# Turning row maxima into shift rows: a transposing DMA in place of TensorE transposes and a VectorE copy

## What is computed

```python
qkv = (x @ Wqkv.T + bqkv).reshape(Bb, Ss, 3, H, HD).transpose(2, 0, 3, 1, 4)
q, k, v = (qkv[0], qkv[1], qkv[2])
attn = jax.nn.softmax(jnp.einsum('bhid,bhjd->bhij', q, k) / jnp.sqrt(jnp.float32(HD)), axis=-1)
...
out = jnp.einsum('bhij,bhjd->bhid', mod, v).transpose(0, 2, 1, 3).reshape(Bb, Ss, Ee)
return out @ Wout.T + bout
```

## Time and profile before

| | |
|---|---|
| median of 3 runs | 988.95 us |
| lowest and highest | 984.64 and 991.41 us |
| the profiled execution | 985.31 us, span 983.5 us |
| mean granted share of the TensorE clock | 0.974 |

### The profile page before, as it was taken

How to read it: one execution, slowest core, us unless ns; L and a number is a source line. 1 busy time by engine, 2 the same in 40 slices (tenths; PEclk the granted TensorE clock), 3 DMA queues, 4 the chain that set the end, 5 groups by cost and what they waited for, 6 DMA issues and landing times. The chain is left out here.

```text
span 983.5 us, 24019 instructions
## 1 busy us (share of the span) xinstructions
PE 910.8 (93%) x6978; PEld 548.8 (56%) x6979; DVE 743.0 (76%) x1546; ACT 536.0 (54%) x1104; POOL 622.0 (63%) x761
## 2 busy tenths in 40 slices
PE   6799999999999999998878998989999999999993
PEld 3233333333333343332314777878888888888882
DVE  7688889898998999899886886685655665655652
ACT  3167787788778777875677653223233233233230
POOL 4314345546556555532445699889988878788785
PEclk9799999999999999998989999999999999999997
DMA  6553171714518162450365896834334334333332
GB/s 214 103 87 77 35 117 56 133 53 89 131 35 163 55 102 64 79 98 13 120 184 161 258 254 180 184 56 73 63 57 55 44 55 55 44 56 54 44 57 30
DMA packets 106768, 93.10 MB, mean 95 GB/s; under 512 B 60025, under 2 KB 99321, under 8 KB 104385
## 3 DMA queue, kind: packets, MB, share of 16 engines
q1 hardware_dynamic: 92000, 71.98, 31.9%
q0 software_dynamic: 14304, 19.15, 12.3%
q10 hardware_dynamic: 384, 0.97, 0.3%
HBM read 49.46 MB, written 38.68 MB: 90 GB/s over the span
## 5 line engine op out<-in xcount | busy, mean ns | idle before, releaser
L1232 DVE TENSOR_REDUCE mx<-bank 128x1 f32<-128x512 f32 x512 | 327.4, 682 | 45.2 <-PE bank L802 40.3
L1122 ACT ACTIVATE arena<-bank 128x512 f32<-128x512 f32 x512 | 277.7, 596 | 70.7 <-PE bank L813 67.0
L1155 ACT ACTIVATE hf<-bank,small 128x256 f32<-128x256 f32 x316 | 133.6, 471 | 262.5 <-PE bank L987 216.5
L677 POOL TENSOR_TENSOR hl<-hf,hh 128x256 f16<-128x256 f32 x316 | 236.5, 1114 | 56.2 <-DVE y_dest L1471 40.8
L1454 DVE CAST hh<-hf 128x256 f16<-128x256 f32 x316 | 178.7, 597 | 114.1 <-ACT hf L1155 108.0
L987 PE MATMUL bank<-hh,arena 128*128 128x256 f16 x1248 | 210.8, 275 | 9.2 <-POOL hl L677 8.2
L802 PE MATMUL bank<-arena 48*128 48x512 f16 x512 | 167.0, 393 | 13.9 <-DVE mx L1232 10.7
L987 PE MATMUL bank<-hl,arena 128*128 128x256 f16 x624 | 171.7, 275 | 0.0
L813 PE MATMUL bank<-arena 49*128 49x512 f16 x512 | 163.2, 388 | 8.5 <-ACT arena L1122 5.8
L685 POOL DMA_INDIRECT out<-y,y_dest x78 | 128.5, 1648 | 20.7 <-issue 17.6
L987 PEld LDWEIGHTS bank<-hh,arena 128*128 x1248 | 122.6, 98 | 32.6 <-issue 14.6
(11 more groups left out here) (215 smaller groups left out, 982.0 us busy)
## 6 DMA issues: line engine op xcount, KB each, us to landing
raw<-in_we SPq DMA_DIRECT2D x16, 1024.0 KB
arena<-parts_dram SPq DMA_DIRECT2D x84, 128.0 KB
parts_dram<-arena SPq DMA_DIRECT2D x64, 128.0 KB, 3.7
xs<-in_pads SPq DMA_DIRECT2D x8, 816.0 KB
arena<-in_xT SPq DMA_DIRECT2D x8, 512.0 KB, 4.6
arena<-in_x SPq DMA_DIRECT2D x8, 512.0 KB, 5.9
out<-rows SPq DMA_DIRECT2D x8, 512.0 KB, 5.0
arena<-parts_dram SPq DMA_DIRECT2D x24, 64.0 KB, 3.0
```

The costliest lines, as they stand in the source:

```text
L677: nc.gpsimd.tensor_tensor(hl[which][:, par, m, :], hf[which][:, m, :], hh[which][:, par, m, :], ALU.subtract).then_inc(lo[which], 1)
L1122: nc.scalar.activation(pr[:, s % TT, n, :], b_bank[no % B_RING][:, :], ACT.Exp, scale=SCALE).then_inc(b_read, 1)
L1155: nc.scalar.activation(hf[which][:, m, :], layer[which][m // 2][:, m % 2 * TS:(m % 2 + 1) * TS], ACT.Relu, bias=bias[which][:, bass.ds(e, ...
L1232: V.tensor_reduce(mx[:, g % 2, s % TT, c:c + 1], a_bank[no % A_RING][:, :], X, ALU.max).then_inc(a_read, 1)
```

## The change

The maxima are laid out as 16 adjacent columns, head by head, in a tile padded with zeros to 128 columns. SP turns that 128 x 128 tile by one transposing DMA from SBUF to SBUF, so that column (head, block) becomes a partition of 128 values, waits for it, and stores eight such partitions to each half of the stack. The four transposes on PE, their use of a PSUM bank and the copy on DVE are gone, and `shift` is [128, 2, 128] in place of [4, 2, 512].

```diff
     i, ahead = SHIFTS_AT[s % SLOTS]
     b = s // SLOTS + ahead
-    return [("mt", i, b)] if 0 <= b < B else []
+    return [(i, b)] if 0 <= b < B else []
...
-    order = [t for s in range(FIRST, LAST) for t in shift_task(s) + tasks(s)]
+    order = [t for s in range(FIRST, LAST) for t in tasks(s)]
...
-    shift = carve(b3_words[:, S + E + VW:S + E + VW + S].bitcast(F16), 0, [G, 2, S])
+    shift = carve(b3_words[:, S + E + VW:S + E + VW + P].bitcast(F16), 0, [P, 2, P])
...
-    mx = sb("mx", [P, 2, TT, G])
-    mxp = sb("mxp", [P, 2, TT, G], F16)
+    mx = sb("mx", [P, 2, G, TT])
+    mxp = sb("mxp", [P, 2, P], F16)
...
         def store_shift(g, b):
-            evicted(sp, ("mt", g, b))
+            n = b * NG + g
+            sp.wait_ge(mx_split, n + 1)
+            sp.wait_ge(bank_cleared, 2)
+            if n >= 2:
+                sp.wait_ge(shift_in, 32 * (n - 1))
+            sp.dma_start(shift[:, g % 2, :], mxp[:, g % 2, :], transpose=True).then_inc(shift_turned, 16)
+            sp.wait_ge(shift_turned, 16 * (n + 1))
             for half in range(2):
                 r = half * ROW_HALF + STACK
-                sp.dma_start(q[r:r + 1, b % 2, 2 * g:2 * g + 2, :], shift[2 * half:2 * half + 2, g % 2, :])\
+                sp.dma_start(q[r:r + 1, b % 2, 2 * g:2 * g + 2, :], shift[half * 2 * TT:(half + 1) * 2 * TT, g % 2, :])\
                     .then_inc(shift_in, 16)
...
-            elif what == "mt":
-                turned_shift = m[0:G, 0:S // 2].bitcast(F16)
-                for t2 in range(TT):
-                    last = nc.tensor.transpose(turned_shift[:, t2 * P:(t2 + 1) * P], mxp[:, i % 2, t2, :], ident[:, :])
...
-            for t in shift_task(s):
-                product(t)
             scores(s, (2, 3))
...
         def split_maxima(g):
             dve.wait_ge(a_read, (g + 1) * TT * G)
-            V.tensor_scalar(mxp[:, g % 2, :, :], mx[:, g % 2, :, :], -1.0 / SHIFT_UNIT, None, ALU.mult).then_inc(mx_split, 1)
+            if g >= 2:
+                dve.wait_ge(shift_turned, 16 * (g - 1))
+            V.tensor_scalar(mxp[:, g % 2, 0:G * TT], mx[:, g % 2, :, :].rearrange("p h t -> p (h t)"), -1.0 / SHIFT_UNIT, None, ALU.mult)\
+                .then_inc(mx_split, 1)
...
-            elif what == "mt":
-                if b * NG + i >= 2:
-                    dve.wait_ge(shift_in, 32 * (b * NG + i - 1))
-                V.tensor_copy(shift[:, i % 2, :], m[0:G, 0:S // 2].bitcast(F16)).then_inc(done, 1)
...
         V.memset(pv_bank[:, :], 0.0).then_inc(bank_cleared, 1)
+        V.memset(mxp[:, :, G * TT:P], 0.0).then_inc(bank_cleared, 1)
```

More of the change, by code:

```diff
@@ L365, in model @@
     a_ready, a_read, b_ready, b_read = sem("a_ready"), sem("a_read"), sem("b_ready"), sem("b_read")
-    mx_split, shift_in = sem("mx_split"), sem("shift_in")
+    mx_split, shift_turned, shift_in = sem("mx_split"), sem("shift_turned"), sem("shift_in")
     slots_free, out_copied = sem("slots_free"), sem("out_copied")
@@ L499, in _ @@
             for t in shift_task(s):
-                store_shift(t[1], t[2])
+                store_shift(*t)
             if s == 1 - SLOTS:
@@ L861, in inputs_ready @@
                 pe.wait_ge(vpart_set, b + 1)
-            elif what == "mt":
-                pe.wait_ge(mx_split, b * NG + i + 1)
-                pe.wait_ge(cleared, 11)
             elif what == "ot":
@@ L1231, in reduce_head @@
             c = column(head_of(n, True))
-            V.tensor_reduce(mx[:, g % 2, s % TT, c:c + 1], a_bank[no % A_RING][:, :], X, ALU.max).then_inc(a_read, 1)
+            V.tensor_reduce(mx[:, g % 2, c, s % TT:s % TT + 1], a_bank[no % A_RING][:, :], X, ALU.max).then_inc(a_read, 1)
         def split_maxima(g):
             dve.wait_ge(a_read, (g + 1) * TT * G)
-            V.tensor_scalar(mxp[:, g % 2, :, :], mx[:, g % 2, :, :], -1.0 / SHIFT_UNIT, None, ALU.mult).then_inc(mx_split, 1)
+            if g >= 2:
+                dve.wait_ge(shift_turned, 16 * (g - 1))
+            V.tensor_scalar(mxp[:, g % 2, 0:G * TT], mx[:, g % 2, :, :].rearrange("p h t -> p (h t)"), -1.0 / SHIFT_UNIT, None, ALU.mult)\
+                .then_inc(mx_split, 1)
         def newton(r, t, m):
@@ L1520, in _ @@
             for t in shift_task(s):
-                split_maxima(t[2] * NG + t[1])
+                split_maxima(t[1] * NG + t[0])
             if scored(s + LEAD):
@@ L1524, in _ @@
                 reduce_head(s + LEAD, 1)
-            for t in shift_task(s):
-                take(t)
             if (at, 0) in ROUTE_AT and 0 <= b - 1 < B:
```

## The result

The changed kernel takes 1003.27 us in the median of four runs (997.98 to 1006.68); the kernel before, beside it on the same chip, 988.31 us (984.64 to 991.41). The ratio is 1.0161, with a 95% interval of 1.0124 to 1.0198: it is 1.6% slower. The profiled execution is the quickest of the four, 997.98 us, its span 996.1 against 983.5 us.

The account below looks back on a forecast made before the run. PE was taken to bound the middle of the attention, DVE close behind. Terms -6.4 - 1.9 - 2.0 + 5.4 - 1.8 = -6.7 us, from 988.9 to 982.2 us; range 974 to 996.

Parts of the forecast that it names:

- The place and the mechanism: Slot 6's transposing DMA queues behind the next batch's stack reads, so PE waits at slot 8, not at 0, 4, 12.
- Rival D: Every group: SBUF-to-SBUF transposing DMA has a longer fixed time; PE waits from 3.5 us on; about 1005 to 1032 us; chance 0.15.
- rival C: Slot 8: wait over 2 us as transposing DMA and stores each queue; six batches x 2.5 us; 994 us; chance 0.15.
- the size of the wait at slot 8: PE waits 1.1 us in batch 4, 0.9 us in the mean over six batches, 5.4 us in all.
- +5.4 -1.8: Slot 8 waits over six batches cost 5.4 us, of which a third, 1.8 us, is taken as given back.
- the 1.8 us given back: While PE stands at slot 8, DVE and ScalarE catch up, so the waits of slots 11 and 12 shrink.
- The fixed times: With free queues: transposing DMA 1.8 us (0.3 for the signal), stores 2.1, plus 0.1; chain 4.0 us from the maxima.
- 6.4 us: PE, slots 2, 6, 10, 14: removing the transposes saves 0.20 us in each of 32 groups.
- 2.0 for VectorE: Removing DVE's copy saves 0.33 us once in each of six middle batches, at slots 11 and 12; 2.0 us.
- The last line of the prediction: Sign of being wrong: a DVE that paces the attention would cut PE's 6.4 us saving and raise DVE's 2.0.
- The waits for the maxima ahead of the transposes: PE idled 2.9 us in two waits before L947; 1.0 us comes back as a wait, so 1.9 us saved.
- order in SyncE's queue: Slot 6: each engine takes one queue's descriptors in ring order, so the transposing DMA lands behind the reads, at 311.7 us.

## Why the prediction was wrong

The forecast was 982.2 us, with a range up to 996; the time is 1003.3. Point by point, by its own steps.

**The place and the mechanism: right.** Everything was to hang on slot 6's transposing DMA meeting the stack reads, with one PE wait at slot 8, and no wait at slots 0, 4 and 12. So it is. Rival D, a transposing DMA that is slow in every group, is out: 2.27 us with free engines, under the 3.5 from which it would decide. It is rival C, the wait at slot 8 over 2 us, that came, and harder than it was priced.

**The step that failed: the size of the wait at slot 8,** 0.9 us in the mean. The waits sum to 15.5 us in six batches, 2.6 in the mean, and slots 7 and 8 together lost 18.8 us, 3.1 a batch, where +5.4 -1.8 stood in the sum. Of the 1.8 us given back, 0.7 is seen: behind the three long waits slot 10 takes 3.47 us in place of 3.70. The parts of the wait in batch 4, where 1.1 us was forecast and 3.27 measured:
- The turn was to land 5.0 us after the maxima and took 6.8. The reads were to start 0.4 us later against the maxima and start 0.9 later: they went 11.9 us ahead of them before and 11.0 after. I had let them clear at 311.0, maxima + 4.3, from two windows of 1 us, and had put the transposing DMA's own part behind that at 0.3 us. The reads did clear in time, the last at maxima + 3.8, and 120 of the turn's 128 packets are through at maxima + 4.1. What had no term in the sum is the rest: the last eight come at maxima + 5.5, behind the instruction packet, and from there to the stores 1.35 us more pass. In batches 1, 2 and 6, without that packet, the turn takes 5.0 to 5.9 us and the wait is 1.4 to 2.3.
- The stores were to take 2.1 us and take 2.55.
- Due it was 6.1 us after the maxima, 0.2 later than counted, since slot 6 of this batch didn't get shorter.

**The fixed times were low.** In the free case the stores go 2.27 us after the turn's issue in place of 1.8. The packets are a little earlier than forecast; the view of the DMA engines from 295.2 to 299.2 us, in slices of 0.1 us, has them from 1.1 to 1.4 us after the issue at 295.40 (the last two slices are a scatter):

```profile
DMA  0000000000000283000000000000000000000097
```

But from the last packet, at 296.8, to SyncE's next issue, at 297.67, are 0.9 us, for which I had allowed 0.3. The same holds for the stores, which by their completion signals land 2.4 us after their issue begins. The free chain is so 2.3 + 2.4 = 4.7 us and not 4.0. The 4.8 us that the prediction worked out by the fixed part in the Trainium skill, page "DMA: Bandwidth & Descriptors", section "Anatomy of one DMA", was nearer, and I had set it aside for a reading of the trace in which the signal was guessed and not seen.

**The clock: not in the sum at all.** Before, the middle of the attention had the full grant, and nothing in its rows showed what a wait of 3 us does. It cost 1.5 us in each of three batches, 4.5 of the 18.8 us.

**The gain: too large.** 6.4 us were counted for PE and 2.0 for VectorE, on the reading that in the middle "a microsecond taken from PE should be a microsecond off the span". It isn't: PE counts as busy while any of its overlapping products runs, also while the next one is held up, and of the four slots with transposes two (6 and 10) wait for VectorE's reduction at the fourth score product, and one (2) for GpSimd. The distance I measured, 1.19 against 0.98 us from L826 to the next product, did shrink to 0.98 in the kernel after (309.31 to 310.29), but the end of the slot didn't move (in batches 2 and 6 it did, by 0.2 us). What the removed work gave is 0.4 us a middle batch and by the ratio 4.8 us in all, of an interval from 1.0 to 8.6. The last line of the prediction named this ("a DVE that turns out to pace the attention"). It could have been worked out from the trace of before: `mxp` is done at 306.74, one reduction behind it ends some 0.6 us later, at 307.3, and the fourth product goes at 307.4, 0.2 behind the third of 307.18. With the third at 306.98 the fourth would still have had to wait. The copy's share was right in size: 0.28 us in slot 11 each batch, 0.33 forecast. The waits for the maxima ahead of the transposes went as forecast. Whether their 1.9 us came back can't be said, as that part of the last batch scatters more.

**Queues.** The prediction put the late landing down to order in SyncE's queue and cited the rule on ring order (the Trainium skill, "DMA: Bandwidth & Descriptors", section "Queues, rings and completion order"). The run with the DMA on ScalarE's queue shows that this isn't what decides here: another queue landed it no sooner. The rule itself, on the order within one queue, isn't contradicted by that.

**Rivals as priced.** C gave 994 us: six waits of 2.5 us, less the full gain of 10.3. The waits were right (15.5 for 15). With the gain as it is, 4.8, and the clock's 4.5 it would have been 988.3 + 15.5 + 4.5 - 4.8 = 1003.5, against 1003.3 measured; with the interval of the gain it is 1000 to 1007, so that it comes this close is luck. Its chance of 0.15 rested on the fall of the DMA share to a half in one microsecond, too thin a view: the share falls while one engine can still be held for more than a microsecond.

**Open.** The last batch took 68.9 us before, 71.3 after and 67.6 to 77.1 in the variants, 72.2 where the only edit was to split the reads; its waits differ from run to run, and no run here tells what sets it. How transfers of different queues share one engine isn't shown; only that the turn from the second queue landed right behind the last read. What makes the 16 KB instruction packets fall into a turn in some batches and not in others isn't known, nor why the same wait brings the low clock in one batch and not in another.

## What to carry to other kernels

A small DMA that someone waits for lives by the load on the engines at its moment, and not by its size or its queue: hold its chain, with the time from last packet to next issue read off a trace, against its due time at the busiest place of the period, and move bulk transfers behind it. Leave room for more than the mean: a single 16 KB packet of another queue went with turns of 3.6 to 4.6 us in place of 2.3. Work taken off the busiest engine is worth something only in slots whose end it sets; read the distance to the next slot's start, not the hole that the work leaves. And a wait in an otherwise full TensorE can cost more than its length, so price a chain that may miss by a few microseconds with what comes after it.

## What was not expected of the hardware

- A transposing DMA of 128 x 128 two-byte elements from SBUF to SBUF takes 1.13 us to issue, with free engines 2.27 us from there to SyncE's next issue, and 5.0 to 7.5 us beside 1.5 MB of reads in 1 KB rows (slot 6, batches 1 to 6); issued from a second queue it landed 4.6 to 7.0 us after the maxima.
- A wait of 3.27 us in a busy PE was followed, 0.8 us after its end, by a granted clock of 0.50 from 320.2 to 323.6 us; a wait of 1.56 us left it at 1.00. Between them both were seen: 1.85 us brought the low clock, 2.25 us in another kernel didn't.
- Once the last packet is through, 0.9 us (free engines) to 1.35 us (other transfers about) pass until the queue that waited for it issues its next DMA, and 3.1 us where a 16 KB instruction packet was in flight (batch 3 with the reads split).
- An instruction packet of 16 KB lasts 0.9 to 1.5 us beside quiet engines and 1.6 to 2.5 us beside the reads, and the 14 turns away from the reads in which one started 1.2 to 2.0 us after the issue took 3.6 to 4.6 us in place of 2.3.
